# A fused state-space and LoRA kernel: a masked gram, a mask and the softplus rows move from SBUF into unused columns of a PSUM bank

## The reference, cut to what matters

```python
z = zxbcdt[..., :DIN]
xBC = zxbcdt[..., DIN:DIN + CONV_DIM]
dt2 = zxbcdt[..., DIN + CONV_DIM:]
dt_fw = jax.nn.softplus(dt2[..., :NH] + dt_bias)
dt_bw = jax.nn.softplus(jnp.flip(dt2[..., NH:], 1) + dt_bias)
xBC = jax.nn.silu(_causal_conv(xBC, conv_w, conv_b))
A = -jnp.exp(A_log)
def step(h, t):                       # forward and backward scan
    dA_t, dBx_t, B_t, C_t = t         # dA = exp(dt * A)
    h = dA_t[:, :, None, None] * h + dBx_t[..., None] * B_t[:, None, None, :]
    y = jnp.einsum('bhpn,bn->bhp', h, C_t)
    return (h, y)
```

## Time and profile before

| | |
|---|---|
| time, median of 3 runs | 2268.3 us |
| the profiled execution: its time, its span | 2268.66 us, 2266.9 us |
| TensorE matmul, weight load | 91%, 82% of the span |
| VectorE, ScalarE, GpSimd | 79%, 67%, 47% |
| granted TensorE clock, mean | 0.98 |

### The profile page before, as it was taken

How to read it: one execution, slowest core, us unless ns; L and a number is a source line. 1 busy time by engine, 2 the same in 40 slices (tenths; PEclk the granted TensorE clock), 3 DMA queues, 4 the chain that set the end, 5 groups by cost and what they waited for, 6 DMA issues and landing times.

```text
span 2266.9 us, 51619 instructions
## 1 busy us (share of the span) xinstructions
PE 2061.0 (91%) x14131; PEld 1865.4 (82%) x14131; DVE 1785.0 (79%) x5073; ACT 1517.0 (67%) x2844; POOL 1074.4 (47%) x1291
## 2 busy tenths in 40 slices
PE   0266999999999999999999999999999999999997
PEld 0144898889888898888988889888898888988887
DVE  7555888888888888888888888888888888888764
ACT  4365777666776666766677667776667766667652
POOL 5664555444554445544454444554445544454331
PEclk9966999999999999999999999999999999999999
DMA  5101121122211222112221122211222112221211
GB/s 173 56 23 39 59 69 43 59 67 67 67 40 61 67 67 67 41 60 67 67 67 40 61 67 67 67 42 59 67 67 67 40 61 67 67 68 35 67 40 34
DMA packets 79030, 136.92 MB, mean 60 GB/s; under 512 B 10560, under 2 KB 52288, under 8 KB 78976
## 3 DMA queue, kind: packets, MB, share of 16 engines
q1 hardware_dynamic: 77536, 130.45, 18.9%
q10 hardware_dynamic: 1440, 5.83, 0.7%
HBM read 59.51 MB, written 76.74 MB: 60 GB/s over the span
## 4 chain that ended last, share of the span: by engine, by line
PE 73%; DVE 11%; issue 8%; ACT 3%; POOL 1%; DVEq 1%; ACTq 0%; POOLq 0%
PE bank L1409 27%; PE bank L1519 5%; PE bank L1509 5%; PE bank L1597 3%; PE bank L1585 3%; PE bank L1569 3%; PE bank L1474 3%; PE bank L1527 2%; DVE ST L1262 2%; PE bank L1447 2%; PE bank L1536 2%; PE bank L1538 2%; PE bank L1616 2%; PE bank L1485 1%; PE bank L1449 1%
## 5 line engine op out<-in xcount | busy, mean ns | idle before, releaser
L1409 PE MATMUL bank<-w_hi,XHI 128*128 128x384 f32 (+1 forms) x1560 | 612.2, 392 | 0.0
L1409 PE MATMUL bank<-w_hi,XLO 128*128 128x384 f32 (+1 forms) x1560 | 530.9, 340 | 0.0
L1409 PE MATMUL bank<-w_lo,XHI 128*128 128x384 f32 (+1 forms) x1560 | 529.9, 340 | 0.0
L1034 DVE SCALAR_TENSOR_TENSOR CX<-bank,cw,CX 128x252 f32<-128x252 f32 (+5 forms) x804 | 326.6, 462 | 66.1 <-ACT CX L830 66.1
L787 POOL TENSOR_TENSOR CB<-CB,CM 48x252 f32<-48x252 f32 (+5 forms) x402 | 292.8, 728 | 111.0 <-ACT CM L815 81.4
L815 ACT ACTIVATE T<-bank 64x512 f32<-64x512 f32 x256 | 152.2, 594 | 275.7 <-PE bank L1509 271.0
L1409 PEld LDWEIGHTS bank<-w_hi,XHI 128*128 128x128 f32 x1560 | 298.2, 191 | 36.3 <-issue 25.1
L1409 PEld LDWEIGHTS bank<-w_lo,XHI 128*128 128x128 f32 x1560 | 295.2, 189 | 10.8
L1409 PEld LDWEIGHTS bank<-w_hi,XLO 128*128 128x128 f32 x1560 | 293.5, 188 | 0.0
L1509 PE MATMUL bank<-VB,W 128*128 128x256 f32 x512 | 142.1, 401 | 91.5 <-DVE W L1099 89.7
L744 POOL TENSOR_TENSOR RS<-VE,half_neg 128x1 f32<-128x1 f32 x65 | 35.6, 547 | 375.4 <-DVE VE L1226 375.4
(11 more groups left out here) (260 smaller groups left out, 5245.7 us busy)
## 6 DMA issues: line engine op xcount, KB each, us to landing
carried<-T SPq DMA_DIRECT2D x65, 512.0 KB, 4.6
T<-carried SPq DMA_DIRECT2D x65, 512.0 KB, 3.9
out<-HB SPq DMA_DIRECT2D x129, 256.0 KB, 3.1
XTC<-in_x SPq DMA_DIRECT2D x64, 128.0 KB, 3.5
w_raw<-in_w_all ACTq DMA_DIRECT2D x8, 584.0 KB, 11.3
tables<-tab SPq DMA_DIRECT2D x8, 560.0 KB, 3.8
TB<-tables SPq DMA_DIRECT2D x64, 70.0 KB, 2.9
carried<-U SPq DMA_DIRECT2D x65, 64.0 KB, 3.5
```

The source lines that it names most:

```text
L1034: inc(STT(CX[:, c, :, s:CS], src[:, :, 0:CS - s], cw[:, c, k:k + 1], CX[:, c, :, s:CS], ALU.mult, ALU.add), "conv")
L1409: ins = mm(bank[:, 0:c1 - c0], xs_[:, 1 - p, k, :], ws[:, k, c0:c1], start=(start and k == 0 and n == 0), stop=(last == k and n == 2))
```

## The change: what it does

Of the tiles named, those that live in SBUF before are moved to columns of `bY` that no matmul writes: `GF` to 280 to 407, a copy of the mask `m_lt` to 408 to 471, the new rows `sp_q` and `sp_u` to 472 to 503, a copy of `negA` to 504 to 507. `sp_z` of some steps overlays the raw dt (256 to 271). In the softplus the rows are dealt out anew so that most operations have one operand in PSUM and at most one in SBUF. ScalarE's exponential writes to PSUM. Three instructions that fill the kept columns come once, ahead of VectorE's first iteration, and one memset of GpSimd goes. TensorE's `grams` waits for `rf=2` in place of `dtc=1`, and `project_out` for `nf=1` too.

```diff
+        GF0 = FC0 + 2 * NH
+        GF = bY[:, GF0:GF0 + 2 * CS].rearrange("p (a t) -> p a t", a=2)
+        lt_keep = bY[:, GF0 + 2 * CS:GF0 + 3 * CS]
+        DT0 = GF0 + 3 * CS
+        dt_raw = bY[:, 4 * CS:FC0].rearrange("p (a d h) -> p d a h", a=2, d=2)
+        sp_z, sp_q, sp_u = (bY[:, c:c + 4 * NH].rearrange("p (d a h) -> p d a h", d=2, a=2) for c in (4 * CS, DT0, DT0 + 4 * NH))
+        nA_keep = bY[:, DT0 + 8 * NH:DT0 + 9 * NH]
...
-                            ins = TS(f["z"], f["u"], 2.0, None, ALU.add)
+                            ins = TS(sp_z, sp_u, 2.0, None, ALU.add)
                         elif j == 3:
-                            ins = dve.reciprocal(f["w"], f["z"])
+                            ins = dve.reciprocal(f["w"], sp_z)
                         elif j == 4:
-                            ins = TT(f["z"], f["u"], f["w"], ALU.mult)
+                            ins = TT(f["z"], sp_u, f["w"], ALU.mult)
                         elif j == 5:
-                            ins = TT(f["w"], f["z"], f["z"], ALU.mult)
+                            ins = TT(sp_u, f["z"], f["z"], ALU.mult)
                         elif j == 6:
-                            ins = TS(f["p"], f["w"], LOG1P[4], None, ALU.mult)
+                            ins = TS(f["p"], sp_u, LOG1P[4], None, ALU.mult)
                         elif j < 10:
-                            ins = STT(f["p"], f["p"], LOG1P[10 - j], f["w"], ALU.add, ALU.mult)
+                            ins = STT(sp_z if j == 9 else f["p"], f["p"], LOG1P[10 - j], sp_u, ALU.add, ALU.mult)
                         elif j == 10:
-                            ins = STT(f["p"], f["p"], LOG1P[0], f["z"], ALU.add, ALU.mult)
+                            ins = STT(sp_q, sp_z, LOG1P[0], f["z"], ALU.add, ALU.mult)
...
-                            ins = TT(f["aa"], f["dt"],
-                                     negA[:, :].unsqueeze(1).unsqueeze(1).broadcast_to([P, 2, 2, NH]), ALU.mult)
+                            ins = TT(sp_u, f["dt"],
+                                     nA_keep.unsqueeze(1).unsqueeze(1).broadcast_to([P, 2, 2, NH]), ALU.mult)
...
-                            inc(TT(RF[:, part, :, :], m_lt[:, :].unsqueeze(1).broadcast_to([P, 2 * NH, CS]),
+                            inc(TT(RF[:, part, :, :], lt_keep.unsqueeze(1).broadcast_to([P, 2 * NH, CS]),
                                    decays(0, part), ALU.mult), "rf")
...
-                                inc(dve.tensor_copy(AS[:, 0], SP16["aa"][:, :, :, :]), "asp")
+                                inc(dve.tensor_copy(AS[:, 0], sp_u), "asp")
...
-                                inc(TT(AS[:, 1], SP16["aa"][:, :, :, :], AS[:, 0].bitcast(F32), ALU.subtract), "asp")
+                                inc(TT(AS[:, 1], sp_u, AS[:, 0].bitcast(F32), ALU.subtract), "asp")
...
+                dve.memset(GF[:, :, 0:1], 0.0).then_inc(kept, 1)
+                dve.tensor_copy(lt_keep, m_lt[:, :]).then_inc(kept, 1)
+                dve.tensor_copy(nA_keep, negA[:, :]).then_inc(kept, 1)
+                dve.wait_ge(kept, 3)
                 iterations(dve, body)
...
-                            wait(pe, r, dtc=1, xs=3, conv=NCONV)
+                            wait(pe, r, rf=2, xs=3, conv=NCONV)
...
-                            wait(pe, r, yte=1, g4=2, dd=1)
+                            wait(pe, r, yte=1, g4=2, dd=1, nf=1)
```

More of the change, by code:

```diff
@@ L106, in build @@
         Mt = sb("Mt", [P, 2 * NH, CS])
-        GF = sb("GF", [P, 2, CS])
         GB = sb("GB", [P, 2, CS])
@@ L243, in _ @@
                 pool.memset(half_neg[:, :], -0.5)
-                pool.memset(GF[:, :, :], 0.0)
                 pool.memset(GB[:, :, :], 0.0)
@@ L526, in build @@
         GT = sb("GT", [P, P])
-        SP16 = {n: sb("sp_" + n, [P, 2, 2, NH]) for n in ("x", "a", "u", "z", "w", "p", "dt", "aa")}
+        SP16 = {n: sb("sp_" + n, [P, 2, 2, NH]) for n in ("x", "a", "w", "z", "p", "dt")}
         DD = sb("DD", [P, 2 * NH])
@@ L567, in build @@
             S[n] = Step(sem(n), c, unit)
+        kept = sem("kept")
         stored = [sem("stored_even"), sem("stored_odd")]
@@ L932, in exp_dt @@
                             wait(act, q, dtc=2)
-                            inc(act.activation(SP16["u"][:, :, :, :], SP16["a"][:, :, :, :], ACT.Exp), "edt")
+                            inc(act.activation(sp_u, SP16["a"][:, :, :, :], ACT.Exp), "edt")
                     def silu_z():
@@ L1046, in softplus @@
                             wait(dve, q - 1, nb=1)
-                            ins = TT(f["x"], bY[:, 256:272].rearrange("p (a d h) -> p d a h", a=2, d=2),
+                            ins = TT(f["x"], dt_raw,
                                      dtb[:, :].unsqueeze(1).unsqueeze(1).broadcast_to([P, 2, 2, NH]), ALU.add)
@@ L1053, in softplus @@
                             wait(dve, q, edt=1)
-                            ins = TS(f["z"], f["u"], 2.0, None, ALU.add)
+                            ins = TS(sp_z, sp_u, 2.0, None, ALU.add)
                         elif j == 3:
-                            ins = dve.reciprocal(f["w"], f["z"])
+                            ins = dve.reciprocal(f["w"], sp_z)
                         elif j == 4:
-                            ins = TT(f["z"], f["u"], f["w"], ALU.mult)
+                            ins = TT(f["z"], sp_u, f["w"], ALU.mult)
                         elif j == 5:
-                            ins = TT(f["w"], f["z"], f["z"], ALU.mult)
+                            ins = TT(sp_u, f["z"], f["z"], ALU.mult)
                         elif j == 6:
-                            ins = TS(f["p"], f["w"], LOG1P[4], None, ALU.mult)
+                            ins = TS(f["p"], sp_u, LOG1P[4], None, ALU.mult)
                         elif j < 10:
-                            ins = STT(f["p"], f["p"], LOG1P[10 - j], f["w"], ALU.add, ALU.mult)
+                            ins = STT(sp_z if j == 9 else f["p"], f["p"], LOG1P[10 - j], sp_u, ALU.add, ALU.mult)
                         elif j == 10:
-                            ins = STT(f["p"], f["p"], LOG1P[0], f["z"], ALU.add, ALU.mult)
+                            ins = STT(sp_q, sp_z, LOG1P[0], f["z"], ALU.add, ALU.mult)
                         elif j == 11:
                             wait(dve, q - 1, nb=1)
-                            ins = STT(f["dt"], f["x"], 0.0, f["p"], ALU.max, ALU.add)
+                            ins = STT(f["dt"], f["x"], 0.0, sp_q, ALU.max, ALU.add)
                         elif j == 12:
-                            ins = TT(f["aa"], f["dt"],
-                                     negA[:, :].unsqueeze(1).unsqueeze(1).broadcast_to([P, 2, 2, NH]), ALU.mult)
+                            ins = TT(sp_u, f["dt"],
+                                     nA_keep.unsqueeze(1).unsqueeze(1).broadcast_to([P, 2, 2, NH]), ALU.mult)
                         inc(ins, "dtc")
```

## The result

The changed kernel takes 2246.96 us, the median of five runs (2244.89 to 2254.29), against 2270.61 for the kernel before in the same session (2266.65 to 2272.2). The ratio is 0.9908, 95% interval 0.9885 to 0.9932. The execution that was profiled took 2244.89 us, its span is 2243.1; before they were 2268.66 and 2266.9. So 23.8 us are to be found between the two traces.

A forecast was written before the change was run, and what follows sets the result against it. The prediction took TensorE's waits at `turn_h` and `lora`, set by VectorE operations held by GpSimd's adds, as the bound. 19.4 - 2.3 + 3 = 20 us off 2268.66 gave 2249; range 2239 to 2270, likeliest case 2243 to 2256.

The forecast's parts named there:

- 10 iterations at 0.48 and 47 at 0.31: Middle iterations, VectorE's run up to `turn_h` and `lora`: savings in us for even-like and odd-like iterations, 19.4 us in all.
- 2.3 us: Loss booked for two bank writes between `final_first` and HWS, 0.02 us each, in 57 iterations.
- the 0.07 booked for `lora`: Part of the 0.48 cap: some 0.07 us by which the first `lora` matmul is late.
- one wholly in SBUF waits for GpSimd's to end: VectorE beside GpSimd: operations wholly in SBUF are held, those with a bank operand run on; j = 7 took 0.67, not 0.17.
- Filling and emptying: Pipeline's filling iterations, last iterations and start: together 3 us gained, an estimate.
- The parts booked at nothing: Shorter NF and RF, GpSimd's GF, and TensorE's new waits at `grams` and `project_out`: all hidden or free.
- that cover: Other work hiding NF, RF and GF from TensorE's path; losing it was said to bring a gain, not a loss.
- (a): Rival: both kinds of iteration reach the 0.48 us cap, `NM` winning or j = 5 not held; 2239 to 2241; chance 0.13.
- (b): Rival: the next GpSimd add catches the next operation, only j = 7 counts; 2257 to 2262; chance 0.15 for 2256 to 2264.
- (c): Rival: dependent steps through the bank from j = 8 to RF grow; 0.06 us per link gives 2278; chance 0.13.
- the rule of the Trainium skill: VectorE's overhead about 60 ns on SBUF, 125 on PSUM; eight links 65 ns longer each, kernel near 2278.
- (d): Rival: GpSimd holds VectorE other than by SBUF inputs, nothing freed; 2268; chance 0.09 shared with the end of (b).

The follow-up runs named there:

- experiment 3: Kernel before with only the square that j = 5 writes and j = 6 to 9 read moved to the bank; gained 0.163 us per iteration.
- experiment 4: Changed kernel with `NM` written as a tensor_scalar, its second input a pointer element; 2251.9 us, 31.177 us per iteration.
- experiment 8: experiment 7 with HWS (`weighted_lo`) moved ahead of the first RF in VectorE's list; 2233.17 us, 30.838 us per iteration.
- experiment 11: Changed kernel run again with no edit; median 2254.03 us, ratio 0.9922, 31.168 us per iteration.
- experiment 2: Kernel before with only GF and the mask in the bank, plus TensorE's two new waits; ratio 0.9993.
- experiment 6: Kernel before with TensorE's two new waits alone (`rf=2` at `grams`, `nf=1` at `project_out`); ratio 1.0000.
- experiment 7: experiment 4 with the square of j = 5 given one bank factor, for one more small operation; 31.002 us per iteration.
- experiment 9: Kernel before with only HWS (`weighted_lo`) moved ahead of the first RF in VectorE's list; 332 us slower.

## Why the prediction was right

**The bound and the mechanism.** `turn_h` fell from 0.387 to 0.116 us; I had named 0.15 or below. HWS is 0.05 ahead of `lora` as said, an iteration 31.167 where I said 31.2, NF and RF 0.68. That VectorE was released by GpSimd's adds is shown by experiments 3 and 4: take a hold away and the time goes, unless the next add catches the next operation.

**The steady part.** 10 iterations at 0.48 and 47 at 0.31 less 2.3 us were 17.1 us in 57, 16.2 in 54. Measured: 16.4, of which 14.7 (0.273 per iteration) lie ahead of `turn_h` and the rest is spread thinly over TensorE's list. That the sum fits so closely is partly luck, since its terms were each off and made up for one another. `NM` was held in 48 of 54 (I had 47 of 57), and there `turn_h` finds TensorE idle for 0.13 us in the mean, for 0.39 over all iterations before: 0.26 gained of the 0.31 booked. In the other six its idle is gone, 0.39 of the 0.48: the 0.07 booked for `lora` did not come, since HWS and its load stayed as close as they were, and the delay there (0.15 us by experiment 8, not 0.07) was left whole. The bank's writes cost 4 to 8 ns, not 20, and from the start of `final_first` to the end of HWS it is 2.142 us in the mean of the 54, 2.144 before: 2.3 us booked as lost, none found.

One reading under the prediction was too wide: "one wholly in SBUF waits for GpSimd's to end". `NM` as a scalar operation in experiment 4 has all its operands in SBUF, ran inside a GpSimd instruction in 63 of 65 instances and was never held (at most 214 ns).

**Filling and emptying.** The term was mis-sized, or can't be told: 3 us booked, 7.4 seen between the two profiled executions, 3.8 the other way in experiment 11 (filling and emptying 271.6 and 299.8 us, against 270.3 and 297.3 before). The clock there varies by more than the term; it can't be read from single traces.

**The parts booked at nothing.** Gram, mask and waits: experiments 2 and 6, 0.9993 and 1.0000. Right in this order of the list, and only in it: "if that cover went, it would be a gain, not a loss" missed that the old place of the mask was one edit away from 330 us.

**The rivals.** (a) needs both `NM` and j = 5 free, and experiment 7 makes that kernel: 31.002, 0.47 less than before, where the rival had 0.48, with next to no wait at `turn_h` (0.005). The change does not reach it, since `NM` is held. (b) is real, and experiment 4 shows it, but it was not what the change met: j = 5 was long in four instances only. (c) is refuted by 178 ns for a write, and the rule of the Trainium skill cited in the prediction with it: bank to bank takes 173 ns where the free operation on SBUF takes 166 to 170, not 65 more. (d) is refuted by the group means: NF and RF at 0.68, j = 7 at 0.16.

## What to carry to other kernels

An operation with two SBUF inputs beside a busy GpSimd is released at an end of GpSimd's, so its cost is not its own length but the place where it lands; freeing one can pass the hold to the next two-input operation (`NM`, then j = 5, here), and only the chain to the last of them counts. Follow that chain to the engine that waits before booking the nanoseconds. And before two steps are swapped, look which GpSimd instructions each two-input operation will then stand beside: a hold that was hidden (RF, 1.23 us) ran over four of them (3.97 us) after one swap.

## What the runs showed of the hardware that I had not expected

- A held VectorE operation need not be let in between GpSimd instructions that follow without a gap: in experiment 9 RF took 3.97 us over four of them in each of 54 iterations; by itself it takes 0.68. In the kernel before it was let in between two (1.23 us).
- A one-element scalar operation on SBUF, its second input a pointer (`NM` of experiment 4), has a mean of 204 ns and at most 214 inside GpSimd's instructions, while the 16-element scalar operation j = 2, one tensor input, is held (0.61 us).
- TensorE's wait of 2.73 us in each iteration was followed by some 6 us at the 1.2 GHz level; that cost about as much again, some 3 us.
- HWS ahead of one RF of 0.68 us, with `lora`'s weight load 0.05 us behind it before, is worth 0.16 to 0.23 us per iteration; moving the rows to the bank gave 0.30.
